# Attention steps taken in pairs, with both layers of an expert tile in one step and a score bank for layer two

## The reference

```python
xn = _layernorm(x, axis=-1)                      # x: (4, 1024, 128)
x = x + _L0_attn_ref(xn, W_q, W_k, W_v, W_o) + _L0_ffn_ref(xn, Wg, gamma, beta, W1, b1, W2, b2)
# attention: H = 16 heads of DK = 8, rotary embedding on Q and K, softmax(Q K / sqrt(8)) V, times W_o.T
# experts: E = 8, top K = 2 of them per token, F = 512
#   xhat = layernorm(xf, eps 1e-6); h = relu((xhat * gamma[e] + beta[e]) @ W1[e] + b1[e])
#   out[e] = h @ W2[e] + b2[e] + xf; y = sum of the two chosen out[e], weighted by a softmax of their scores
```

## Time and profile before

| | |
|---|---|
| time, median of 3 runs | 619.22 us (618.95 to 620.86) |
| the profiled execution | 618.98 us, its span 617.1 us |
| PE busy | 566.1 us (92%) |
| ACT busy | 502.2 us (81%) |
| DVE busy | 303.2 us (49%) |
| POOL busy | 246.7 us (40%) |

### The profile page before, as it was taken

The page is one execution under the profiler, slowest core; times in us unless marked ns, Lnnn a source line. Parts: engine busy times, 40 slices in busy tenths (PEclk is TensorE's granted clock), DMA queues, the critical chain, the costliest instruction groups (busy, mean ns, idle before and its releaser), DMA issues.

```text
span 617.1 us, 12160 instructions
## 1 busy us (share of the span) xinstructions
PE 566.1 (92%) x4620; PEld 239.3 (39%) x4620; DVE 303.2 (49%) x1002; ACT 502.2 (81%) x552; POOL 246.7 (40%) x303
## 2 busy tenths in 40 slices
PE   8899959788999999999999999999999999989774
PEld 6333202123455444444445444434434544434111
DVE  4865785774434343455453333355444443333582
ACT  2699978688877888788887888887888788878993
POOL 4399700109855323464623333255633233231000
PEclk9999998799999999999999999999999999999997
DMA  6158410013443434332343353432243334340721
GB/s 245 31 157 238 127 34 2 1 71 115 163 138 141 139 133 155 117 137 98 129 165 109 142 176 112 144 145 97 105 175 130 144 133 160 119 163 19 289 92 38
DMA packets 35583, 77.56 MB, mean 126 GB/s; under 512 B 6576, under 2 KB 16864, under 8 KB 35008
## 3 DMA queue, kind: packets, MB, share of 16 engines
q1 hardware_dynamic: 30160, 65.80, 29.7%
q0 software_dynamic: 4544, 9.32, 5.1%
q10 hardware_dynamic: 816, 1.61, 0.7%
HBM read 17.36 MB, written 8.85 MB: 42 GB/s over the span
## 4 chain that ended last, share of the span: by engine, by line
PE 72%; ACT 13%; DVE 9%; issue 4%; DMA 1%; ACTq 0%; DVEq 0%
PE acc L673 28%; ACT ring L886 13%; PE aside_bank L717 12%; PE sc L639 10%; PE aside_bank L727 10%; PE aside_bank L706 3%; PE aside_bank L566 2%; PE aside_bank L736 2%; DVE work L1255 1%; DVE blocks L1055 1%; PE aside_bank L550 1%; DVE xn L1188 1%; DVE rotated L1232 1%; PE sc L566 1%; DMA wr<-L_attn_W_k 1%
## 5 line engine op out<-in xcount | busy, mean ns | idle before, releaser
L886 ACT ACTIVATE ring<-sc 128x1024 f32<-128x1024 f32 x512 | 489.0, 1040 | 90.0 <-PE sc L639 80.3
L673 PE MATMUL acc<-ring,v 128*9 128x512 f32 x2048 | 271.4, 602 | 26.2 <-ACT ring L886 12.1
L491 POOL DMA_INDIRECT work<-normed,token x71 | 71.5, 1008 | 222.6 <-DVE work L1249 197.3
L1255 DVE TENSOR_SCALAR work<-aside_bank,xn 128x128 f32<-128x128 f32 x284 | 79.9, 344 | 113.4 <-PE aside_bank L717 111.0
L639 PEld LDWEIGHTS sc<-qs,ks 32*128 32x128 f16 x1024 | 26.0, 91 | 229.3 <-ACT ring L886 202.6
L639 PE MATMUL sc<-qs,ks 32*128 32x512 f16 x1024 | 102.3, 388 | 4.4 <-ACT ring L886 2.4
L501 POOL DMA_INDIRECT token_out<-work,token x71 | 71.1, 1001 | 42.4 <-DVE work L1249 19.4
L717 PE MATMUL aside_bank<-work,xn 128*128 128x128 f32 x568 | 82.1, 288 | 1.1 <-DVE rotated L1232 0.6
L717 PEld LDWEIGHTS aside_bank<-work,xn 128*128 128x128 f32 x568 | 68.7, 191 | 17.4 <-issue 17.4
L727 PE MATMUL aside_bank<-xn,work 128*128 128x128 f32 x568 | 75.1, 275 | 0.0
L727 PEld LDWEIGHTS aside_bank<-xn,work 128*128 128x128 f32 x568 | 71.4, 196 | 0.3 <-DVE work L1255 0.3
(11 more groups left out here) (184 smaller groups left out, 329.6 us busy)
## 6 DMA issues: line engine op xcount, KB each, us to landing
xn<-w_all SPq DMA_DIRECT2D x71, 579.0 KB
w_all<-L_ffn_W SPq DMA_DIRECT2D x16, 256.0 KB, 5.1
qs<-hl SPq DMA_DIRECT2D x60, 64.0 KB
ks<-hl SPq DMA_DIRECT2D x60, 64.0 KB
x<-L_attn_x SPq DMA_DIRECT2D x4, 512.0 KB, 8.4
normed<-xn SPq DMA_DIRECT2D x4, 512.0 KB, 3.4
xn<-token_out SPq DMA_DIRECT2D x2, 1024.0 KB, 6.0
w_all<-token_out SPq DMA_DIRECT2D x2, 1024.0 KB, 10.6
```

The source lines that it names most:

```text
L491: pool.indirect_dma_start(out=xt[t % TILE_BUFFERS], out_offset=None, in_=xh_d[:, :], in_offset=bass.IndirectOffsetOnAxis(ap=token[:, 0, t: ...
L673: last = nc.tensor.matmul(acc[32 * j:32 * j + VW, :], v9[:, b, kb, 4 * g + j, :], ring[:, (2 * n + j // 2) % UNITS, j % 2, :], start=(kb = ...
L886: nc.scalar.activation(ring[:, (2 * n + u) % UNITS, :, :], sc[score_pair(2 * n + u)][:, :].rearrange("p (h c) -> p h c", h=2), ACT.Exp, sc ...
L1255: last = nc.vector.tensor_scalar(hT[t % 2][:, c, :], bank[0][:, c * P:(c + 1) * P], w_tile[t % 3][:, B1_AT + c:B1_AT + c + 1], 0.0, ALU.ad ...
```

## The change

From step 52 on, steps are taken in pairs (`PAIRS`). In the even step of a pair PE makes the next scores and then, where the step is not taken by other aside work, layer one of tile k, turns the rows of tile k+1 and runs layer two of tile k-1 (`tile`). Turned rows and layer two go into the score pair that is free then (`SPARE`), not into `aside_bank`. The weighing of the even step is put behind the next step's scores, so the odd step has both weighings. `score_homes` works out which pair each score unit uses and how many exps must be done before; the scores of an odd step in a tile pair keep off the spare pair.

- `ring` grows from four units to six.
- DVE's `tail` is split into `take_sums` and `divide`; relu and the rows and columns of a tile stand between them.
- Owners are worked out at step 29, apart from `place`; gates at 39 instead of 46. The first two marks go from steps 27 and 28 to 32 and 33, the others and the inverts to new steps; tokens from 49 to 47.
- The projections of the second batch go from steps 38, 44, 48, 51 to 28, 49, 50, 54; those of later batches and of the output move by some steps. POOL's first split stands with the other three behind the fourth gather instead of ahead of the gathers.
- W1 is no longer kept in SBUF. `weights` issues two DMAs per tile, W1 from HBM and the rest from `w_rest`, into one of four buffers.
- Merges start one step later.

```diff
+def score_homes():
+    home, need, spare, order = [], [], {}, [0, 1]
+    last = {0: -1, 1: -1, 2: -1}
+    for n in range(STEPS):
+        if n == 2:
+            order = [2] + order
+        before = n - 2 if n - 2 in TILE_AT else None
+        for u in range(2):
+            pair = next(k for k in order if before is None or k != spare[before])
+            order.remove(pair)
+            order.append(pair)
+            home.append(pair)
+            need.append(last[pair] + 1)
+            last[pair] = 2 * n + u
+        if n - 1 in TILE_AT:
+            spare[n - 1] = order[0]
+            SPARE_NEED[n - 1] = last[order[0]] + 1
+    return home, need, spare
...
-            split(1, 0)
...
-            def layer_two(t):
-                pe.wait_ge(bank_taken[0], USE["one", t])
-                enter_bank(0, "two", t)
-                if t + 1 < SLOT_TILES:
-                    turn_tile(t + 1)
...
+            def layer_two_and_turn(k, n):
+                home = sc[SPARE[n]]
+                pe.wait_ge(e_ok, SPARE_NEED[n])
+                if k + 1 < SLOT_TILES:
+                    last = turn_tile(home, k + 1)
+                if k > 0:
+                    t = k - 1
+                    pe.wait_ge(bank_taken[0], USE["one", t])
+                    for c in range(FC):
+                        last = nc.tensor.matmul(home[:, P:2 * P], hT[t % 2][:, c, :],
+                                                w_tile[t % WEIGHT_BUFFERS][:, W2_AT + c * D:W2_AT + (c + 1) * D],
+                                                start=(c == 0), stop=(c == FC - 1))
+                last.then_inc(tile_full, 1)
+
+            def tile(k, n):
+                if k < SLOT_TILES:
+                    layer_one(k)
+                layer_two_and_turn(k, n)
...
-                        pe.wait_ge(e_ok, 2 * n + 1)
+                        pe.wait_ge(e_ok, NEED[2 * n + 3])
+                        if n - 2 in TILE_AT:
+                            pe.wait_ge(tile_taken, TILE_AT[n - 2] + 1)
...
-                        weigh(n)
+                        if n - 1 in PAIRS:
+                            weigh(n - 1)
+                        if n not in PAIRS:
+                            weigh(n)
...
+            def rows_and_columns(k, n):
+                home = sc[SPARE[n]]
+                v.wait_ge(tile_full, k + 1)
...
                 if n % KB == 0 and n > 0:
-                    tail(n // KB - 1)
+                    take_sums(n // KB - 1)
+                if TILE_AT.get(n, SLOT_TILES) < SLOT_TILES:
+                    relu(TILE_AT[n])
+                if n in TILE_AT:
+                    rows_and_columns(TILE_AT[n], n)
+                if n % KB == 0 and n > 0:
+                    divide(n // KB - 1)
```

## The result

The changed kernel takes 588.88 us (median of 4 runs, 587.15 to 589.35), the one before 619.96 beside it. The ratio is 0.949 (95% interval 0.947 to 0.952). The gain is 31 us where 20 were forecast, so the question is where the other 11 came from.

The account below looks back on a forecast made before the run. The prediction took PE to set the pace in the middle and waits to hold the front. From 618.98 us it took 11.4 in the middle and 8.3 in the front, giving 599.3, forecast 599 us, range 588 to 612.

Parts of the forecast that it names:

- Rival (1): Whole kernel: everything hides, 4.61 us per pair and ACT's late starts and squares at 2 us, so 587; chance 0.13.
- (a): Middle, ACT: exps start late on issue, 8.2 us before; with half of ACT's slack gone, 3 us charged.
- (c): Middle, ACT: squares wait for sums on POOL; 2.5 us charged for eight squares.
- The pair: Middle, PE: a full pair of steps with a tile takes 4.66 us instead of 4.85, 70 times.
- The wait for both exps: Odd step's scores wait for both exps, 2.43 us after the even scores, hidden behind 2.44 to 2.49 of PE work.
- rival (3): Tile pairs: ACT's return path is longer than 2.43 us, each 0.1 costing 7 us; 628 at 2.9; chance 0.06.
- The first and last tile pair: Middle: the two tile pairs with only part of the tile work take 3.7 us each.
- ACT's lost slack: Middle, ACT: late starts, squares and their wait on POOL come out, charged 3 + 5 + 2.5 us, bounds 0 to 20.
- (b): Middle, ACT: 16 squares of 0.63 us, half of it charged, 5 us.
- Pairs without a tile: Middle: 21 pairs bound by four ACT slots, 3.68 us each, 77.3 us in all.
- The front: Scores of step 22 to those of 53: moved DVE work removes PE's waits, 72.4 to 64.1 us, so -8.3.
- Weights: Middle: two transfers per tile, one from HBM, have 8.6 us until the columns want them; no cost.

Follow-up runs that it names:

- The layers apart: The changed kernel with the turned tile and layer two moved to the odd step, behind its scores, layer one staying in the even step: 671.67 us.
- the extra exp: The changed kernel with one extra 8-column exp on ACT between the two exps of odd, or else even, steps of tile pairs: 598.80 and 593.38 us.
- the second execution: The changed kernel run again with nothing changed, on a chip where the kernel before took 615.96 us: 585.34 us, ratio 0.949.

## Why the prediction came out as it did

The mechanism was right and the sum too high. The middle came out 8 us below the forecast and the front 3. Rival (1), with 587 and a chance of 0.13, stands nearest to the measured time, but only its pair of 4.61 came true: it had (a) to (c) at 2 us, and it left the front as forecast.

**The pair: right, its size too cautious.** "I take 4.66" was the mis-sized term. The sum from the intervals inside a group, 4.61, was right and even 0.02 high (turned tile to layer two 0.11, not 0.13, and both weighings 1.84, not 1.85). I had added 0.05 for waits in mid-stream that cost nothing. At 4.59 the 70 pairs are 5 us less. Two weighings in a row take 1.84, one alone 0.98. The Trainium skill (TensorEngine Tiling (Array Packing), Key Properties) says that a change of the tiling mode drains TensorE and a change of the tile alone does not. The trace agrees: neither the second weighing nor the turned tile behind layer one, where the shape stays, costs anything extra.

**The wait for both exps: right, and exact.** 2.43 of return path against PE's 2.44 to 2.49 was the forecast. Measured: 2.42 to 2.43 for the path, and PE's work in front of it no more than that. The layers apart and the extra exp show that the wait is real. An exp that is 0.10 later costs 0.10 per pair, so rival (3) had the right mechanism and lacked only the lateness that it named, 0.34.

**The first and last tile pair: wrong.** They were put at 3.7 each and took 4.58. With half the tile work PE is done early, but the odd scores still wait 2.42 for both exps, a wait that the prediction had worked out for full pairs and left out here: 1.8 us too little.

**ACT's lost slack: forecast 10.5, with pauses 13.5.** The steps' periods beyond 2.42 in tile steps, 2.16 in odd ones and 1.51 in those without a tile add up to about 9.5 us, and to about 5.5 in the second execution. Late starts, (a), are the difference: 4 us in one and nothing in the other, with 3 charged, so how near this term came to the measured one is in part chance. The squares, (b) and (c), cost 3.3 of it in the later two batches, as their moving shows, with 7.5 charged; there are 12 squares in all and not the 16 that I counted. The charge for waiting on POOL (2.5) was wrong: two squares of eight waited, 0.2 us each. What a square costs depends on the gap it falls into, and I had charged half for all.

**Pairs without a tile: right.** Forecast 3.68, measured 1.51 + 2.16 = 3.67.

**The front: right cause, mis-sized.** Forecast 64.1, measured 61.3. Two of the three prices in "18 at 1.84, 13 with an aside at 2.3" were too high. The eight steps with an invert took 16.7 us and not 18.4: at full clock such a step costs 1.92 where nothing waits (rows of the kernel before below), since an invert takes PE 0.6 and not 1.0. The steps without an aside took 1.74 on average and not 1.84, for one that follows an aside can be as short as 1.51. The other five asides took 0.6 us more than charged. The new wait at step 48, forecast 1.1, is there: PE is idle 1.63 before that weighing, and the step takes 3.00, 1.16 above 1.84.

```profile
99.56 0.40 PE L639 MATMUL sc<-qs,ks 32*128 32x512 f16 x4
99.88 0.68 PE L699 MATMUL aside_bank<-xn 128*128 128x142 bf16 x8
100.49 1.04 PE L673 MATMUL acc<-ring,v 128*9 128x512 f32 x8
101.47 0.40 PE L639 MATMUL sc<-qs,ks 32*128 32x512 f16 x4
```

**Weights: right for a reason that was thinner than I wrote.** 8.6 us were counted, and the columns did start 9.1 after the issue, with no wait. But the copies that were waited for in the kernel with three buffers landed 3.4 to 6.2 us after their issue, and that eats much of it. "No cost" holds only with the fourth buffer, and the prediction did not say so.

**Tail.** 0.6 us longer; PE's idle before the last weighing grew from 2.38 to 2.88. No run tested this.

## What to carry to other kernels

Where two kinds of matmul alternate on PE, put the same kinds together: here an avoided change of tile shape was worth 0.10 to 0.12 us, and two per pair, with a shorter start of the turned tile, took 5% off the pair. When a buffer is borrowed for it, work out the return path that the lender now waits for (here 2.43 us through ACT), and put at least as much PE work in front: with it the loan was free, without it each pair took 5.74 us instead of 4.59. Count the room of a copy up to its first reader: here that was DVE's columns and not layer one, and one buffer less cost the whole gain. An engine brought to the edge like this makes small things count by their place: the squares, in the gap instead of out of it, gave another half per cent. And look at regular steps before totals: late starts that come and go moved the middle by 4 to 6 us, more than some of the changes tested.

## What the runs showed of the hardware

- Weight loads and waits inside a run of matmuls of one shape cost nothing measurable: turned tile and layer two follow layer one at 0.99 and 0.11 us, the interval of the matmuls themselves, though a semaphore wait stands before each (one trace of the changed kernel, every full pair alike).
- Two copies of 256 and 323 KB, issued 0.5 to 0.8 us apart, landed 3.4 to 6.2 us after the first issue (median 4.0 of the 43 that were waited for). With both from SBUF the columns that waited started 3.2 to 5.8 after it (median 3.9 of 47), and the source, SBUF or HBM, changed a pair by less than 0.1 us. The last packet of the two ended 3.1 to 5.7 us after the first issue (median 3.5), that of the same 579 KB as one copy in the kernel before 2.5 to 4.7 (median 2.8).
- A tiny activation of 8 columns takes a slot of 0.10 us between exps of 1024 columns, half of its 0.20 us of recorded time.
